# A GRU and a conditioned transformer layer on one core: prologue reordered, modulations spread, first q and k begun in the last GRU block, exp table asked for early

## The reference, cut to what matters

```python
for t in range(128):                      # GRU, h starts as cond
    gi, gh = x[:, t] @ W_ih + b_ih, h @ W_hh + b_hh
    r, z = sigmoid(gi_r + gh_r), sigmoid(gi_z + gh_z)
    n = tanh(gi_n + r * gh_n)
    h = (1 - z) * n + z * h
x = x + hs
shift1, scale1, gate1, shift2, scale2, gate2 = split(cond @ ada_w + ada_b, 6)
x1 = ln(x) * (1 + scale1) + shift1
q, k, v = split(x1 @ qkv_w + qkv_b)       # 16 heads of 128, 128 tokens
a = softmax(q k^T / sqrt(128)) v
x2 = x + gate1 * (a @ out_w + out_b)
y = x2 + gate2 * (gelu((ln(x2) * (1 + scale2) + shift2) @ ffn_w1 + ffn_b1) @ ffn_w2 + ffn_b2)
return x + y                              # all in float32
```

## Time and profile before

| | |
|---|---|
| runs, us | 801.28, 801.40, 802.28 (median 801.4) |
| the profiled execution's own time, us | 801.32 |
| its span, first to last instruction, us | 799.4 |
| PE busy | 753.2 us, 94% of the span |
| DVE, ACT, POOL busy | 580.4, 470.9, 101.2 us |
| mean granted TensorE clock | 0.899 |

### The profile page before, as it was taken

One profiled execution on the slowest core, in us unless ns is written; L12 is line 12 of the kernel. 1 busy time (PEld: TensorE's weight loads), 2 busy tenths in 40 slices (PEclk: granted clock), 3 DMA queues, 4 the chain that ended last, 5 costly groups with the idle time before them and its releaser, 6 DMA issues.

```text
span 799.4 us, 24458 instructions
## 1 busy us (share of the span) xinstructions
PE 753.2 (94%) x10068; PEld 532.7 (67%) x10068; DVE 580.4 (73%) x1548; ACT 470.9 (59%) x1564; POOL 101.2 (13%) x121
## 2 busy tenths in 40 slices
PE   6888989889888889999999999999999999999998
PEld 5777777777777656666666666666667666644445
DVE  5677777777777567777788887788877888853543
ACT  4344444444443266667777667777677776766454
POOL 0221222222222200000030010020010300100130
PEclk9977665766877599999999999999999999999999
DMA  6121121112111012222222222222222222210001
GB/s 221 43 96 42 43 81 43 43 42 78 45 35 37 2 27 41 40 42 41 41 41 40 41 41 41 41 41 41 41 41 41 41 41 41 41 27 26 1 27 53
DMA packets 76566, 36.65 MB, mean 46 GB/s; under 512 B 70395, under 2 KB 73127, under 8 KB 76327
## 3 DMA queue, kind: packets, MB, share of 16 engines
q1 hardware_dynamic: 75879, 33.52, 18.3%
q10 hardware_dynamic: 576, 1.57, 0.6%
HBM read 16.20 MB, written 2.10 MB: 23 GB/s over the span
## 4 chain that ended last, share of the span: by engine, by line
PE 83%; ACT 6%; DVE 5%; DMA 2%; issue 2%; SPq 1%; DVEq 0%; ACTq 0%
PE bank L366 19%; PE bank L367 19%; PE bank L368 19%; PE bank L439 12%; PE bank L386 7%; PE bank L446 5%; DVE h_hi L998 3%; DMA pT_lo<-p_lo 2%; ACT zg L763 2%; ACT prob L812 1%; ACT nu L766 1%; PE bank L373 1%; PE bank L414 1%; ACT zz L764 1%; SPq L257 1%
## 5 line engine op out<-in xcount | busy, mean ns | idle before, releaser
L439 PE MATMUL bank<-h_hi,whh_hi 128*128 128x16 f16 x1536 | 112.8, 177 | 29.0 <-DVE h_hi L998 28.5
L439 PEld LDWEIGHTS bank<-h_hi,whh_hi 128*128 128x128 f16 x1536 | 92.7, 101 | 65.6 <-DVE h_hi L998 65.6
L366 PE MATMUL bank<-y_hi,w_hi 128*128 128x512 f16 (+2 forms) x324 | 122.6, 379 | 1.3 <-ACT hf L845 1.3
L367 PE MATMUL bank<-y_hi,w_lo 128*128 128x512 f16 (+2 forms) x324 | 122.6, 379 | 0.0
L368 PE MATMUL bank<-y_lo,w_hi 128*128 128x512 f16 (+2 forms) x324 | 122.3, 379 | 0.0
L439 PE MATMUL bank<-h_hi,whh_lo 128*128 128x16 f16 x1536 | 110.6, 176 | 0.0
L761 ACT ACTIVATE zr<-bank 128x32 f32<-128x32 f32 x128 | 25.7, 201 | 130.1 <-PE bank L446 130.1
L812 ACT ACTIVATE prob<-bank,nmx 128x128 f32<-128x128 f32 x256 | 90.4, 365 | 19.9 <-DVE nmx L1074 19.9
L439 PEld LDWEIGHTS bank<-h_hi,whh_lo 128*128 128x128 f16 x1536 | 93.4, 101 | 0.1
L366 PE MATMUL bank<-w_hi,y_hi 128*128 128x128 f16 x512 | 89.1, 219 | 0.0
L367 PE MATMUL bank<-w_hi,y_lo 128*128 128x128 f16 x512 | 89.1, 219 | 0.0
(11 more groups left out here) (142 smaller groups left out, 2092.4 us busy)
## 6 DMA issues: line engine op xcount, KB each, us to landing
stage<-in_weights SPq DMA_DIRECT2D x16, 640.0 KB, 4.1
x<-in_x SPq DMA_DIRECT2D x16, 128.0 KB, 4.3
out<-yT SPq DMA_DIRECT2D x3, 512.0 KB, 2.6
adar<-in_ada_r SPq DMA_DIRECT2D x1, 1024.0 KB, 7.2
pT_hi<-p_hi SPq DMA_TRANSPOSE x64, 2.4
pT_lo<-p_lo SPq DMA_TRANSPOSE x64, 2.4
wih<-in_W_ih ACTq DMA_DIRECT2D x2, 384.0 KB, 4.0
whh<-in_W_hh ACTq DMA_DIRECT2D x2, 384.0 KB, 6.1
```

The source lines that it names most:

```text
L366: mm(ps, w[0], a[0], start=start, stop=False, skip_group_check=True)
L367: mm(ps, w[1], a[0], start=False, stop=False, skip_group_check=True)
L439: nc.tensor.matmul(out(m0 + m), half[:, k, w], h_hi[:, k * B:(k + 1) * B, 1], start=False, stop=False, skip_group_check=True)
```

## The change

- Prologue: SP loads x's block 0 before `small` (the biases and cond), and holds the loads of x's block 1, of the modulation weights, of the first weight pieces and of x's block 2 until W_hh's two halves have landed. ACT converts x before W_ih, DVE too. PE takes the input products by half of W_ih's columns.
- GRU: the row modulation of block 0 goes to four steps (`ROW_TILES`), one float32 product each; its `x_bias` goes to step 0, its input products follow `share_0`. The eight tiles of the other modulation go to step 0 of blocks 7 to 14, one each. In block 15, steps 1, 2, 3, 4, 6 and 7 get two products each of q and k of head 0, over the first 112 tokens.
- Transition: 8 tokens of block 14 and 8 of block 15 remain for q and k of head 0. Five of the six products of head 1's q over 120 tokens stand around `rows_back`, in bank 4; the sixth and the last 8 tokens after `values(0)`.
- ACT runs one `Exp` on a spare tile after the last GRU step; the table load stands before it.
- `tin` and `yT` are gone: PE turns `xr2` itself, `sum_group` writes into `xr2`, and the output's layout follows it (runs of 512 B and 2 KB in place of 1 KB and 4 KB).
- `up(2)` writes bank 4 and waits for the norm's last tile in place of the first GELU.

```diff
+ROW_TILES = {1: (0, 0), 2: (0, 1), 4: (1, 0), 5: (1, 1)}
+ADA_AT = 3
...
             sp.dma_start(grow[:, :], gate_rows).then_inc(grow_in, 16)
+            load_x(0)
             sp.dma_start(small[:, :], cols_in).then_inc(small_in, 16)
-            for n in range(3):
-                load_x(n)
-            load_pieces(0)
+            sp.wait_ge(whh_in[0], 16)
+            load_x(1)
+            sp.wait_ge(whh_in[1], 16)
             sp.dma_start(adaw[:, :, :], ada_a).then_inc(adaw_in, 16)
             sp.dma_start(adab[:, :], ada_b[0:2 * D].unsqueeze(0).broadcast_to([P, 2 * D])).then_inc(adaw_in, 16)
+            load_pieces(0)
+            load_x(2)
...
-                sp.dma_start(out[:, NG - 1, j, :, :], yT[:, NG - 1, j, :, :]).then_inc(y_out, 16)
+                b = (NG - 1) * QUAD + j
+                sp.dma_start(out[:, :, b, :], xr2[:, :, b, :]).then_inc(y_out, 16)
...
             for k in range(KD):
-                if k == 0:
-                    pe.wait_ge(xt_lo, 1)
-                pe.wait_ge(wih_l, 2 * k + 2)
-                x_products(0, [(m, k, i) for m in range(GM) for i in range(3)])
+                for half in range(2):
+                    pe.wait_ge(wih_l, 2 * k + half + 1)
+                    x_products(0, [(m, k, i) for m in range(half * GM // 2, (half + 1) * GM // 2) for i in range(3)])
...
+            early, middle, last = slice(0, T - 2 * BS), slice(T - 2 * BS, T - BS), slice(T - BS, T)
+            before = slice(0, T - BS)
+
+            def tall_parts(order, which, head, t):
+
+                w = slice((which * H + head) * DH, (which * H + head + 1) * DH)
+                ps = bank[4 * head + which][:, :].rearrange("p (j t) -> p j t", j=QUAD)[:, :, t]
+                for k, i in order:
+                    wq, y = ((wq_hi, y_hi), (wq_lo, y_hi), (wq_hi, y_lo))[i]
+                    mm = nc.tensor.matmul(ps, wq[:, k, w], y[:, k, 0:QUAD, t], start=t.start == 0 and (k, i) == (0, 0),
+                                          stop=(k, i) == (KD - 1, 2), skip_group_check=True)
+                return mm
+
+            tall_rest = [(k, i) for k in range(KD) for i in range(3)]
+            tall_at = {1: (0, 0), 2: (0, 2), 3: (0, 4), 4: (1, 0), 6: (1, 2), 7: (1, 4)}
...
+            share_0 = (0, 0, 0, 2, 11, 15, 19, 27, 36)
...
-                    elif r == NBL - 1 and s in (1, 2, 3, 4):
-                        if s == 1:
-                            pe.wait_ge(rest_in, 16)
-                        modulation(range(2 * s + 2, 2 * s + 4))
+                    elif r == NBL - 1 and s in tall_at:
+                        which, first = tall_at[s]
+                        if s == 1:
+                            pe.wait_ge(piece_lo, QKV_PIECES)
+                            pe.wait_ge(lb_lo, NBL - 2)
+                        tall_parts(tall_rest[first:first + 2], which, 0, early)
+                    elif G1 <= r - ADA_AT < ADA and s == 0:
+                        modulation(r - ADA_AT)
             rows_T(NBL - 1)
             pe.wait_ge(lb_lo, NBL - 1)
-            first_head(0, before, True)
+            tall_parts(tall_rest, 0, 0, middle)
+            tall_parts(tall_rest, 1, 0, middle)
+            pe.wait_ge(ada_add, 1)
+            tall_parts(tall_rest[0:3], 0, 1, before)
             rows_back(NBL - 1)
-            first_head(1, before, True)
+            tall_parts(tall_rest[3:5], 0, 1, before)
             pe.wait_ge(lb_lo, NBL)
...
-                if t > 1:
+                if t == 2:
+                    pe.wait_ge(ln_y, 2 * (NG - 1))
+                elif t > 2:
                     pe.wait_ge(f_gelu, t - 1)
...
+                if d == 0:
+                    tall_parts(tall_rest[5:], 0, 1, before)
+                    tall_parts(tall_rest, 0, 1, last).then_inc(q_mm, 1)
+                elif d < HEADS - 1:
                     queries(d + 1)
...
+            nc.scalar.activation(spare[:, :], nhalf[:, :], ACT.Exp)
             y_high(NBL - 1)
```

More of the change, by code:

```diff
@@ L219, in build, with up_bank @@
         xr_v = xr[:, :, :, :].rearrange("p k n (b t) -> p k b n t", b=B)
+        def up_bank(t):
+            return bank[4 if t == 2 else t % 2]
         def by_block(ap):
@@ L476, in _ @@
                     if r < NBL - 1:
-                        if s == 1:
+                        if s == (1 if r > 0 else 0):
                             x_bias(r + 1)
@@ L480, in _ @@
                             pe.wait_ge(xt_lo, r + 2)
-                        x_products(r + 1, products[share[s]:share[s + 1]])
-                    if r == 0 and s == 3:
-                        pe.wait_ge(adaw_in, 32)
-                        pe.wait_ge(small_in, 16)
-                        row_modulation(0)
-                    elif r == 0 and s == 5:
-                        row_modulation(1)
-                    elif r == NBL - 1 and s in (1, 2, 3, 4):
-                        if s == 1:
+                        now = share if r > 0 else share_0
@@ L490, in _ @@
                             pe.wait_ge(rest_in, 16)
-                        modulation(range(2 * s + 2, 2 * s + 4))
+                        modulation(r - ADA_AT)
             rows_T(NBL - 1)
-            def first_head(which, t, start):
-                w = slice(which * H * DH, which * H * DH + DH)
-                ps = bank[which][:, :].rearrange("p (j t) -> p j t", j=QUAD)[:, :, t]
-                for k in range(KD):
-                    mm = product(ps, (wq_hi[:, k, w], wq_lo[:, k, w]), (y_hi[:, k, 0:QUAD, t], y_lo[:, k, 0:QUAD, t]),
-                                 start and k == 0, k == KD - 1)
-                return mm
@@ L572, in tall @@
                 g, head = d // H, d % H
-                if d == 0:
-                    mm = first_head(which, last, False)
-                else:
-                    pe.wait_ge(free, d)
-                    w = slice((which * H + head) * DH, (which * H + head + 1) * DH)
-                    for k in range(KD):
-                        mm = product(bank[which][:, :], (wq_hi[:, k, w], wq_lo[:, k, w]),
-                                     (y_hi[:, k, g * QUAD:(g + 1) * QUAD, :], y_lo[:, k, g * QUAD:(g + 1) * QUAD, :]),
-                                     k == 0, k == KD - 1)
+                pe.wait_ge(free, d)
+                w = slice((which * H + head) * DH, (which * H + head + 1) * DH)
+                for k in range(KD):
+                    mm = product(bank[which][:, :], (wq_hi[:, k, w], wq_lo[:, k, w]),
+                                 (y_hi[:, k, g * QUAD:(g + 1) * QUAD, :], y_lo[:, k, g * QUAD:(g + 1) * QUAD, :]),
+                                 k == 0, k == KD - 1)
                 mm.then_inc(ready, 1)
@@ L668, in last_down @@
                     mm.then_inc(f_down, 1)
-            queries(0)
+            tall_parts(tall_rest, 0, 0, last).then_inc(q_mm, 1)
+            tall_parts(tall_rest, 1, 0, last).then_inc(k_mm, 1)
             for d in range(HEADS):
```

94 lines of the change are left out of this document (46 added, 48 removed).

## The result

The changed kernel takes 797.1 us (median of 4 runs, 796.80 to 797.31), the kernel before in the same set 801.84 (4 runs, 801.28 to 802.55): ratio 0.9943, 95% interval 0.9928 to 0.9959, so 4.7 us or 0.6% faster. The spans of the profiled executions are 794.9 and 799.4 us, the mean granted clock is 0.899 in both. The forecast was 796.0, range 793.0 to 799.0.

A forecast was written before the change was run, and what follows sets the result against it. PE was taken to bound the kernel, with 83% of the path. Terms 1.2 + 0.5 + 1.9 - 1.0 + 2.85 + 0 - 0.1 = 5.35 us off 801.32 gave 795.97, forecast 796.0, range 793.0 to 799.0.

The forecast's parts named there:

- PE's order at the transition: After the GRU, the early q and k products let the softmax maxima start 1.74 us earlier.
- Prologue, 1.2: Start: x lands about 4.7, PE's first input product starts about 6.1 instead of 7.3; gain 1.2 us, between 0.45 and 1.65.
- Block 0, 0.5: Row modulation spread over four steps gains 0.5 us (0 to 0.9); nothing counted for x's block 2 landing late.
- Tiles, -1.0: Step 0 of blocks 7 to 14: five hide their tile, two pay 0.56 us, one a little; cost about 1.0.
- Block 15, 1.9: Seven steps lose the modulation tiles; the q and k products replacing them fit PE's wait; gain 1.9 us, 1.4 to 2.0.
- Transition, 2.85: GRU to attention: maxima 1.74 us earlier plus about 1.1 from hiding the table load; gain 2.85 us, bounds 1.1 to 4.8.
- Feed-forward, 0: `up(2)` starts without its 1.26 us wait, but the stall moves behind it, before `down(0)`; gain 0, at most 0.1.
- Output, -0.1: Last stores in 512 B runs need twice the packets; cost 0.1 us, between 0 and 0.5.
- the clock rises: Rival: added work in step 0 and block 15 lifts the clock; 792.6 us or between; chance 0.19, shared with DMA sooner.
- Swallowed: Rival: the table's 1.1 us at the transition becomes another wait, 797.1; with x's block 2 late about 798.5; chance 0.19.
- the slower rival: Rival: the clock falls, blocks 1 to 14 take 16.60 us each and all tiles cost 0.56; 804.8 us; chance 0.05.
- the last rival: Rival: no change; x lands with `small` as before and tiles cost all block 15 saves; 800.5 us; chance 0.07.

The follow-up runs named there:

- The other trace with the old code: The kernel before with only the eight modulation tiles moved from block 15 to step 0 of blocks 7 to 14: 799.25 us, ratio 0.9984.

## Why the prediction came out as it did

The forecast of 796.0 was 1.1 us too low. Block 15 and the table came as forecast. The other terms were off by up to 1 us in both directions: prologue -0.5, block 0 -1.0, tiles +0.9, PE's order at the transition -0.7, from the exponential to `attend(0)` +1.0, output -0.8. They cancelled in part, so that the total came this near is partly luck.

- **Prologue, 1.2.** Mis-sized in this pair: PE's first product at 6.65, not 6.1. Of the 0.55 missing, 0.39 is x, which came at 5.09 where I took 4.7. The rest is small: I counted half a conversion on ACT ahead of `wih_lo`; what stands there is `xb_lo` on DVE, 0.42 us, beside which ACT's half runs. With x at 4.28 PE starts no sooner, so x's transfer is not the only bound: what DVE does ahead of `xb_lo` is another. Over seven traces the first `h_hi` comes 1.3 us sooner than in the two of the old prologue, but part of that is the level during the input products, not the order.
- **Block 0, 0.5.** Failed in this pair of traces, with the sign turned (-0.49). The step that failed is "I count nothing" for x's block 2: it landed at 17 us, ACT waited 1.71 us for it, and 0.77 of that was paid, within the range's "up to 1 us of loss". What was said of the row modulation itself held. Without what step 2 has over 2.03 us, block 0 would take 16.3 and 16.4 us in the two traces where the third product met the higher level and no other step was long, and 16.7 to 16.9 in the four where it met the lower one: 0.5 to 0.6 and 0.1 to 0.3 under the 16.95 of before (an estimate from the steps of these traces). The other trace with the old code shows the price of the lower level there: its first two products stand in a step of 3.72 us, and block 0 takes 18.14.
- **Tiles, -1.0.** Mis-sized: 0.07, and 0 within the spread of the traces. (The sum itself was loose: twice 0.56 and a little is over 1.1, not 1.0.) I charged a tile with its 0.94 us, half of the eight records of the earlier trace rows, against the wait that was shown. At the lower level the next step's first product started 0.71 us behind the tile's start, while the tile's records go on to 0.87 (block 7, 127.77 to 128.48), and the step grew by 0.1, not 0.56. At the higher level the tile takes 0.52 (block 8), PE's wait shrank from 0.65 to 0.30, and the step did not grow. Computed twice, the tiles cost 5.3 us in the trace, so the first had used up the room.
- **Block 15, 1.9.** Right: 1.90 in the pair, 1.95 by the tiles alone.
- **Transition, 2.85.** The sum 3.18 is near, the parts are not. The table's 1.1 is right (1.14; 1.15 with the exponential taken out). The Trainium skill ("ScalarE: Activation LUTs", "Rules for kernel authors") budgets about 2.7 us for a switch. Here the trace differs from it: the load's row has 1.28 in both places and taking it off the path was worth 1.14, so the price of 2.7 is refuted for this path. Of the 1.74 for PE's order 1.05 came. k's low half ended where I had it; the step that failed is `values(0)`, which I priced at 1.3 us "at the higher level" and which took 2.48, nearly all at the lower. So `scores(0)` started 8.39 us behind the last `h_hi` where I had 7.84, and `mx` then stood behind `v_lo` on DVE, which I had not counted. The level rose 7.8 us after the last `h_hi`, before 6.3 (279.4 less 273.06) and without the early q 10.3. PE's idle time from the last `h_hi` to `values(0)` is 1.5, 0.9 and 3.6 us in these three. The eight other traces keep the order: 5.9 us with 0.9 us idle in the other old kernel, 7.1 to 9.3 with 1.5 in the seven that have the early q. So the more PE idled there the later the level rose; that the idle time is the cause is argued, since no run changes it alone. The other 0.99, from the exponential to `attend(0)`, can't be put down to the change: this stretch is 7.0 to 8.3 us in eight other traces of the changed code and 8.03 with the old code, so 8.62 was a long one.
- **Feed-forward, 0.** Right: taking the edit back changes the 92.12 us by nothing. The stall did not go all behind `up(2)` (0.47 of 1.4); most of it went ahead of the attend.
- **Output, -0.1.** Mis-sized: -0.9. I had twice the packets and no price for issuing them. Each issue takes SP 0.2 to 0.3 us longer, the four stand in a row at the end of the span, and the last lands 0.56 us later after its start.

Of the rivals, "the clock rises" fell: from the first to the last `h_hi` the lower level holds 0.60 of the time before and 0.59 after, and adding tiles cost time. "Swallowed" named x's block 2 rightly, and its 797.1 is the measured time, but by luck: the table's gain was not swallowed. The time of the slower rival, 804.8, needed blocks 1 to 14 to lengthen; they did not. The 800.5 of the last rival does not follow from its two conditions: without the prologue's 1.2 and with the tiles costing all of block 15's 1.9, the other terms still give 798.1.

## What to carry to other kernels

When a load is moved to the front, count each conversion that stands in one row behind it on one engine, and then ask which load it pushed back and who waits for that: x's block 2 was late here, and the gates' rows once x went ahead of them. Work given to an engine's wait was free here as long as it fitted, and the second tile was paid nearly in full; computing a piece twice shows how much room is left. The last four stores were on the path one by one, so the length of their runs counted.

## What was not expected of the hardware

- Stores of 128 KB in runs of 512 B took 0.53 to 0.62 us each to issue and landed 0.66 us apart; in runs of 1 KB they took 0.33 and landed 0.52 apart, as fast as the sums came.
- The same code gives a first `h_hi` between 12.2 and 13.4 us and a first `attend` 7.0 to 8.3 us after the exponential, from one execution to the next. A part of the first spread is TensorE's level, which rose during the input products in some traces and after them in others. One pair of traces does not show a difference under 1 us in these stretches; it takes more of them.
- `values(0)`, 24 products, took 1.5 us in the kernel before, at 2.4 GHz, and 2.5 us in the changed one, where the level was still 1.2 GHz: the earlier start put it into the time of the lower level, which took back a part of what that start was worth.
